# Constant products on TensorE ahead of long waits, host-laid weights and context, and a new step order in a one-core decoder layer

## What is computed

```python
x = x + attn(layernorm(x), gamma)        # softmax over -gamma * |xi - xj|^2, keys = values = the input itself
x = x + xattn(layernorm(x), ctx, ctx)    # 16 heads of width 8, alibi term slope_h * (i - j), Wq, Wk, Wv, Wo and biases
x = x + ffn(layernorm(x))                # 8 experts, the two with the largest router logits summed, W_e (128 x 128), b_e

mask = one_hot(top_k(softmax(h @ router_w.T + router_b), 2)).sum(-2)
out  = einsum('bse,ehd,bsd->bsh', mask, expert_w, h) + mask @ expert_b
```

## Time and profile before

| | |
|---|---|
| median of three runs | 304.29 us (303.43 to 306.56) |
| the profiled execution | 304.62 us, its span 302.8 us |
| instructions | 3232 |
| ScalarE, GpSimd busy | 111.9 us (37%), 61.6 us (20%) |
| DMA queues | 19.25 MB, 64 GB/s in the mean |

### The profile page before, as it was taken

How to read it: one execution, slowest core, us unless ns; L and a number is a source line. 1 busy time by engine, 2 the same in 40 slices (tenths; PEclk the granted TensorE clock), 3 DMA queues, 4 the chain that set the end, 5 groups by cost and what they waited for, 6 DMA issues and landing times.

```text
span 302.8 us, 3232 instructions
## 1 busy us (share of the span) xinstructions
PE 221.5 (73%) x1065; PEld 110.6 (37%) x1065; DVE 163.4 (54%) x405; ACT 111.9 (37%) x206; POOL 61.6 (20%) x114
## 2 busy tenths in 40 slices
PE   0858374688959899679989977987955799833194
PEld 0328251332823337623334663324334142223031
DVE  2167566379063678938476893825686240134060
ACT  1363351620155785145475415434102604500000
POOL 6160521200030000368000032800010250010080
PEclk9999788755589999959999996997985579995569
DMA  3790038500103510033532002451100400000521
GB/s 76 215 252 4 4 112 161 130 1 2 45 0 104 104 36 0 9 78 120 129 63 68 0 10 69 162 121 35 35 0 13 140 0 3 0 0 0 126 83 35
DMA packets 26409, 19.25 MB, mean 64 GB/s; under 512 B 12249, under 2 KB 25025, under 8 KB 26305
## 3 DMA queue, kind: packets, MB, share of 16 engines
q1 hardware_dynamic: 26393, 19.05, 24.5%
HBM read 13.64 MB, written 5.41 MB: 63 GB/s over the span
## 4 chain that ended last, share of the span: by engine, by line
PE 54%; DVE 22%; issue 9%; ACT 8%; DMA 3%; POOL 2%; SPq 0%; ACTq 0%; DVEq 0%; POOLq 0%
PE bank L1028 11%; PE bank L844 7%; DVE nm L752 6%; PE bank L986 5%; PE bank L887 5%; PE bank L984 5%; PE bank L943 5%; PE bank L904 4%; PE bank L964 3%; ACT pt L601 2%; PE bank L917 2%; DVE y L654 2%; DVE st L644 2%; PE bank L969 2%; ACT w L546 2%
## 5 line engine op out<-in xcount | busy, mean ns | idle before, releaser
L752 DVE TENSOR_REDUCE nm<-bank 128x3 f32<-128x462 f32 x88 | 50.3, 618 | 24.7 <-PE bank L943 23.6
L601 ACT ACTIVATE pt<-bank 128x512 f32<-128x512 f32 x80 | 44.1, 595 | 23.9 <-PE bank L964 11.0
L943 PE MATMUL bank<-kA,qs 128*128 128x308 bf16 (+1 forms) x172 | 33.0, 302 | 8.5 <-DVE nm L752 5.2
L436 POOL TENSOR_SCALAR ve<-mv 128x4 f32<-128x4 f32 x12 | 2.4, 204 | 174.4 <-DVE mv L647 174.3
L1028 PE MATMUL bank<-ym,ewT 128*128 128x512 f32 x64 | 32.4, 664 | 6.2 <-DVE ym L823 6.2
L823 DVE TENSOR_TENSOR ym<-mask_all,y3T 128x512 f32<-128x512 bf16 x16 | 21.6, 1409 | 26.6 <-DMA mask_all<-e_scratch 26.6
L512 POOL TENSOR_TENSOR ym<-mask_all,y3T 128x512 f32<-128x512 bf16 x16 | 25.5, 1624 | 40.1 <-DMA mask_all<-e_scratch 40.1
L964 PE MATMUL bank<-qs,kB 128*128 128x512 bf16 x64 | 26.0, 466 | 5.4 <-ACT pt L601 2.6
L887 PE MATMUL bank<-y1Tg,y1T 128*128 128x512 f32 x32 | 21.0, 746 | 7.9 <-ACT w L538 5.1
L844 PE MATMUL bank<-ident,y 128*128 128x128 f32 x48 | 10.9, 369 | 21.6 <-DVE y L654 21.1
L943 PEld LDWEIGHTS bank<-kA,qs 128*128 128x128 bf16 x172 | 13.9, 105 | 29.6 <-DVE nm L752 19.0
(11 more groups left out here) (145 smaller groups left out, 289.7 us busy)
## 6 DMA issues: line engine op xcount, KB each, us to landing
mask_all<-e_scratch SPq DMA_DIRECT2D x8, 512.0 KB, 4.8
qs<-q_scratch SPq DMA_DIRECT2D x8, 384.0 KB, 5.1
q_scratch<-qpart SPq DMA_DIRECT2D x4, 384.0 KB, 2.5
xs<-in_x_dram SPq DMA_DIRECT2D x4, 256.0 KB, 10.1
q_scratch<-qpart SPq DMA_DIRECT2D x4, 256.0 KB, 2.2
out_dram<-ob SPq DMA_DIRECT2D x4, 256.0 KB, 4.3
kA<-k_scratch SPq DMA_DIRECT2D x8, 120.0 KB, 3.9
kB<-k_scratch SPq DMA_DIRECT2D x8, 120.0 KB, 2.6
```

Source lines behind the costliest of these rows:

```text
L601: nc.scalar.activation(pt[:, n % PT_RING, :], ST[n % 2][:, :], ACT.Exp).then_inc(exps, 1)
L752: v.tensor_reduce(negated[:, GROUP * g:GROUP * g + heads], MX[n % 2][:, 0:heads * J].rearrange("p (s j) -> p s j", s=heads), AX.X, ALU.max ...
L943: last = mm(MX[n % 2][:, at * J:(at + heads) * J], qs[:, b % 2, a, tile(t)], kA[:, s:s + heads, a, 0:J], start=True, stop=True)
```

## The change

Four edits go together.

1. The host lays out the weights, biases and context as the matmuls want them. Five transfers take the place of the 18; the transposes, their copies and two memsets of padding are gone. The second element of x is loaded third, the expert weights and biases last.
2. The TensorE step `keys:0` stands directly behind `y1T:0` and waits for the weights and the context alone. VectorE's `weights:0` (memsets of the value and key buffers) stands ahead of `dist:0`.
3. In most TensorE steps the wait on free banks now comes first, then `warm(bank, step)`, then the wait on the data. `warm` issues products of a constant tile (128x128 by 128x512, bf16, all ones) into the bank that the step will overwrite. A table gives their number for 25 steps, 154 in all.
4. `ORDER` is another text for every engine.

```diff
+WARM = {
+    "y1T:0": 16, "probs:0": 12, "y2T:0": 16, "query:0": 4, "y1T:1": 5, "maxima:0": 13, "scores:0": 3, "y2T:1": 1,
+    "divide:0.0": 1, "y3T:0": 2, "mask:0": 8, "y2T:2": 3, "route:1": 3, "mask:1": 11, "scores:2": 1, "y3T:2": 5,
+    "route:2": 1, "mask:2": 5, "scores:3": 9, "experts:2": 1, "wo:3": 1, "y3T:3": 13, "mask:3": 4,
+    "experts:3": 14, "fT:3": 2,
 }
...
             load(xs[:, 0], x[0].rearrange("(t p) d -> p t d", p=P), x_in[0])
             load(gam[:, :], gamma.partition_broadcast(P), gamma_in)
...
+            load(xs[:, 1], x[1].rearrange("(t p) d -> p t d", p=P), x_in[1])
+            load(wT[:, :, :], proj, weights_in)
+            load(cols[:, :], rows, weights_in)
+            load(ctxT[:, :, :], ctxT_in, ctx_in)
             load(kA[:, :, :, :], k_aug[0], kaug_in)
             load(kB[:, :, :, :], k_aug[1], kaug_in)
...
+            load(ebin[:, :], expert_b, expert_in)
+            load(ewT[:, :, :], expert_w, expert_in)
...
             v = nc.vector
+            v.memset(idle[:, :], 1.0).then_inc(idle_set, 1)
...
         def _(pe):
             mm = nc.tensor.matmul
-            pe.wait_ge(consts, 5)
+            pe.wait_ge(idle_set, 1)
+
+            def warm(bank_, step):
+
+                for _ in range(WARM.get(step, 0)):
+                    mm(bank_[:, :], idle[:, 0:P], idle[:, :], start=True, stop=True)
...
-            def weights(b, _):
+            def keys(b, _):
                 pe.wait_ge(weights_in, W_LOADS * ONE)
-                pe.wait_ge(ctx_in, 5 * ONE)
-                turn(ST[0], lambda i: wraw[:, i, :])
-                turn(ST[1], lambda i: ewraw[:, i, :])
-                turn(MX[0], lambda i: ewraw[:, 4 + i, :])
-                nc.tensor.transpose(YV[:, 0:P], rwraw[:, :], ident[:, :])
-                turn(YM, lambda i: ctx_m[:, i, :])
-                for i in range(B):
-                    last = nc.tensor.transpose(MX[1][:, 32 * i:32 * i + 32], ctx_t[:, i, :], ident[0:32, 0:32])
-                last.then_inc(setup_ps, 1)
-
-            def keys(b, _):
-                pe.wait_ge(setup_sb, 6)
+                pe.wait_ge(ctx_in, ONE)
...
             def y2T_(b, _):
+                pe.wait_ge(pT_sb, T * (b + 1))
+                warm(A1, f"y2T:{b}")
                 pe.wait_ge(normed[1], b + 1)
-                pe.wait_ge(pT_sb, T * (b + 1))
                 turn(A1, lambda t: y2[:, t, :]).then_inc(y2T_ps, 1)
...
             def maxima(b, k):
                 if k == 0:
+                    if b == 0:
+                        pe.wait_ge(setup_sb, 2)
+                    if b >= 1:
+                        pe.wait_ge(mT_sb, b)
+                        pe.wait_ge(maxed, b * GROUPS)
+                    warm(MX[b * GROUPS % 2], f"maxima:{b}")
                     pe.wait_ge(kA_in, 2 * ONE * (b + 1))
                     pe.wait_ge(qs_in, 2 * ONE * (b + 1))
...
             def mask(b, _):
+                pe.wait_ge(y3T_sb, b + 1)
+                warm(YM, f"mask:{b}")
                 pe.wait_ge(mask_ready, b + 1)
                 turn(col16(YM), lambda t: maskp[:, t, :], ident16).then_inc(mask_ps, 1)
 
             def experts(b, _):
+                warm(YV, f"experts:{b}")
                 pe.wait_ge(mask_sb, b + 1)
                 if b == 0:
                     pe.wait_ge(bias_ready, 1)
```

More of the change, by code:

```diff
@@ L50 @@
     "scalar": """
[L51 to L60, removed]
@@ L66 @@
[L66 to L74, removed]
+        stats1:0 y1:0 weights:0 dist:0 rowmax:0 keys:0 gather:0 y2:0 stats1:1 y1:1 query:0 dist:1 rowmax:1
@@ L75 @@
+        divide:1.0 divide:1.1 maxima:2.8 maxima:2.9 wo:1 maxima:2.10 mcat:2 y3:1 gather:3 route:1 y2:3 select:1
+        query:3 store:1 divide:2.0 maxima:3.0 maxima:3.1 maxima:3.2 maxima:3.3 maxima:3.4 maxima:3.5 divide:2.1
+        maxima:3.6 maxima:3.7 wo:2 maxima:3.8 y3:2 maxima:3.9 maxima:3.10 mcat:3 route:2 select:2 store:2
+        divide:3.0 divide:3.1 wo:3 y3:3 route:3 select:3 store:3
     """,
     "tensor": """
-        y1T:0 dist:0 probs:0.0 probs:0.1 probs:0.2 probs:0.3 self:0 weights:0 y2T:0 query:0 keys:0 y1T:1 dist:1
@@ L78 @@
[L78 to L87, removed]
@@ L88 @@
-        maxima:2.10 probs:3.3 self:3 y3T:1 mT:2 route:1 mask:1 scores:2.0 y2T:3 scores:2.1 query:3 scores:2.2
-        scores:2.3 scores:2.4 scores:2.5 experts:1 scores:2.6 values:2.0 values:2.1 scores:2.7 maxima:3.0 fT:1
-        scores:2.8 maxima:3.1 scores:2.9 maxima:3.2 scores:2.10 divide:2.0 scores:2.11 maxima:3.3 values:2.2
-        maxima:3.4 values:2.3 maxima:3.5 divide:2.1 maxima:3.6 aoT:2 maxima:3.7 wo:2 maxima:3.8 maxima:3.9 y3T:2
+        y1T:0 keys:0 dist:0 probs:0.0 probs:0.1 probs:0.2 probs:0.3 self:0 y2T:0 query:0 y1T:1 dist:1 maxima:0.0
@@ new lines @@
+        probs:2.1 divide:0.1 probs:2.2 maxima:1.9 aoT:0 maxima:1.10 wo:0 probs:2.3 mT:1 self:2 y3T:0 scores:1.0
+        route:0 scores:1.1 scores:1.2 mask:0 y2T:2 query:2 scores:1.3 scores:1.4 y1T:3 scores:1.5 scores:1.6
+        experts:0 dist:3 maxima:2.0 values:1.0 maxima:2.1 fT:0 scores:1.7 maxima:2.2 values:1.1 maxima:2.3
+        probs:3.0 scores:1.8 maxima:2.4 scores:1.9 maxima:2.5 scores:1.10 maxima:2.6 scores:1.11 values:1.2
+        maxima:2.7 values:1.3 divide:1.0 maxima:2.8 divide:1.1 probs:3.1 aoT:1 probs:3.2 maxima:2.9 wo:1
@@ L94 @@
-        scores:3.11 values:3.2 values:3.3 divide:3.1 aoT:3 wo:3 y3T:3 route:3 mask:3 experts:3 fT:3
-    """,
+        experts:2 values:3.0 scores:3.6 values:3.1 scores:3.7 fT:2 scores:3.8 scores:3.9 scores:3.10 scores:3.11
+        values:3.2 values:3.3 divide:3.0 divide:3.1 aoT:3 wo:3 y3T:3 route:3 mask:3 experts:3 fT:3
+    """,
+}
+WARM = {
[4 rows of a table added]
 }
@@ L1007, in y3T_ @@
             def y3T_(b, _):
+                warm(YM, f"y3T:{b}")
                 pe.wait_ge(normed[2], b + 1)
```

175 lines of the change are left out of this document (95 added, 80 removed).

## The result

The changed kernel takes **294.76 us** (median of 4 runs, 294.32 to 296.19) against 305.05 for the kernel before, measured beside it (303.43 to 306.56). The ratio is 0.967, 95% interval 0.961 to 0.974. The gain is 10.3 us; the forecast was 22.6 us and its range ended at 291. The profiled execution took 294.3 us, with a span of 292.2. In this document the ratios leave out executions more than 1.5% above the fastest of their kernel and the medians keep them; without them the medians would be lower by 0.4 us (no products), 0.5 (order before), 0.2 (memsets early), 0.7 (tail order) and 1.2 (first 70 products).

A forecast was written before the change was run, and what follows sets the result against it. TensorE, busy 221.5 of 302.8 us with 96 us at half clock, was taken as the bound, besides setup and a few waits. Terms summed to -22.6 us (14.6 clock, 8 order and setup): 282.0 us, range 273 to 291.

The forecast's parts named there:

- Start to y2T:0: Kernel start through y2T:0: no gain, -1 to +3 us; key products hide under the memsets, first row maximum at 14.65.
- Rival 4: At the start, the inputs or the memsets hold back dist:0: +3 us, 285; chance 0.05.
- From the start to query:1: Everything up to query:1's end: done 14.8 us earlier, with the 22 maxima ending at 64.0.
- The scores of element 0 to self:2: From element 0's scores to self:2: +1.8 us, as values:0.2 waits for ScalarE's pvs; TensorE's work otherwise the same.
- Element 1: Stretch of element 1: -2 us, score products filling mask:0's wait of 3.18 us.
- element 2: Stretch of element 2: -5.0 us, from filled waits at mask:1 and ahead of maxima:3.0 and less half clock.
- Element 2's end: Route, y3T, ten scores and experts of element 2: -3.5 us, from full clock and scores bound by ScalarE.
- The clock term: Part of the forecast gain, over the whole kernel, that hangs on the clock: 14.6 us.
- Rival 1: In the maxima and self:1, the clock falls in thin stretches: costs 4.5 us, 286.5; chance 0.20.
- Rivals 2 and 6: Whole kernel: clock hardly holds, 296.6, chance 0.07; or constant operand cannot raise it, no chance of its own.
- rival 5: Whole kernel slower: constant products stand in front of ready work, a third uncovered, 317.6 us; chance 0.03.
- rival 3: No loss at values:0.2 and values:3.2, last experts at full clock: 276 us; chance 0.23.

The follow-up runs named there:

- no products: The changed kernel without any constant product, keeping its order, host layout and loads: 307.05 us, ratio 1.003 to the kernel before.
- order before: The changed kernel with the step order of the kernel before on all engines, keeping constant products and host layout: 299.44 us, ratio 0.976.
- memsets early: The changed kernel with VectorE's three long memsets moved into its idle time at the start: 291.72 us, ratio 0.954.
- tail order: The changed kernel with the order of the kernel before on TensorE and ScalarE from experts:2 on: 291.04 us, ratio 0.951.
- first 70 products: The changed kernel with only the 70 constant products up to y2T:1, the later 84 left out: 305.08 us, ratio 0.994.
- the copy first: The changed kernel with ScalarE's copy of values:0.1 (pvs) ahead of the four ReLUs of dist:2: 293.81 us, ratio 0.963.
- the order before in this place: The changed kernel with its new order up to query:1 and the order of the kernel before from there on: 287.85 us, ratio 0.942.
- the kernel with more products: New order to query:1 and self:3 to experts:2, old order elsewhere, early memsets, more constant products at y2T:0, y3T:3, mask:3, experts:3: 282.58 us, ratio 0.926.
- three moves: The changed kernel with early memsets, values:0.1's copy ahead of dist:2, and the order of the kernel before from experts:2 on: 286.86 us, ratio 0.941.

## Why the prediction was wrong, by its own steps

**Start to y2T:0** (0 forecast, +1.4 measured). The memsets were seen, and the first maximum was placed at 14.65 (15.19 measured). What was not followed is that a later first maximum makes TensorE wait, and that its clock then falls. Rival 4 (memsets hold back the start, +3 us) thus came true in part; taking the memsets out of the way gave 3.0.

**From the start to query:1** (-14.8, measured -14.6). Right in sum, by luck in part: the 1.4 us lost at the start are among the 14.6, so behind y2T:0 the kernel gained 16.0. The first maximum was 1.5 us late, and the 22 maxima with what stands between them ended 12.1 us later, where 13.7 had been counted (50.3 to 64.0). The split between clock and order was off too: without products the stretch is already 10.8 us shorter, against the 8.1 that the prediction left to the order; the products add 3.7, not 6.7.

**The scores of element 0 to self:2** (+1.8, measured +5.7). This is the first step that failed. It priced the `pvs` wait at its length (2.1 us, 2.08 measured) and stopped there. Moving the copy alone takes 3.7 us out of the stretch: 2.1 for the wait and 1.6 for the half clock behind it. Of the other 2.0 us, with the copy first, TensorE's waits are only 0.3 (1.5 before, 1.8 then) and the transposes of mT:1, which stood behind self:2 before, 0.4; the rest is longer busy time of TensorE (31.5 against 29.8 us in all, both at full clock), and its cause stays open. So "TensorE's work is the same" is not quite right for this stretch either. The queries from DRAM, the condition named at the prediction's end, come late only with the order before in this place (1.27 us); with them in time, in the kernel with more products, that order needs 32.2 us.

**Element 1** (-2, measured +1.2) and **element 2** (-5.0, measured -1.6). The waits that were to go did go, but others came. TensorE's waits in the kernel before from 124.3 to 177.4 us, and the same piece of work after, from 115.4 to 169.7 (us in total, times, longest):

```profile
PE bank L844 <- DVE maskp L813: 3.2, 1, 3.2
PE bank L844 <- DVE y L654: 0.5, 1, 0.5
PE bank L887 <- ACT w L538: 0.5, 1, 0.5
PE bank L964 <- ACT pt L601: 0.5, 2, 0.3
PE bank L844 <- DVE ao L775: 0.4, 1, 0.4
```

```profile
PE bank L952 <- ACT pt L584: 2.6, 3, 1.5
PE bank L974 <- ACT pvs L514: 1.7, 1, 1.7
PE bank L833 <- DVE ao L759: 1.0, 2, 0.5
PE bank L900 <- ACT y2T L514: 0.8, 1, 0.8
PE bank L952 <- DMA qs<-m_scratch: 0.6, 1, 0.6
```

These are the five largest of each. The mask wait of 3.2 us is gone, but where the other four sum to 1.9 us, the five of after sum to 6.7; over all releasers it is 6.0 before and 8.1 after. The new ones are waits for exponentials queued behind ScalarE's query work, for a `pvs` that ScalarE makes behind the last exponentials and the copy of probs:3.0, for other copies. With the order before in this place the stretch takes 52.9 us, 1.4 less. The stretch to wo:2 is alike, but milder: before, 3.2 for the mask, 2.8 for the queries and 2.7 in small ones; after, no wait above 0.8 us, but eight releasers whose waits add to 6.0, of which the largest three:

```profile
PE bank L952 <- ACT pt L584: 1.3, 3, 0.6
PE bank L928 <- DVE nm L736: 1.2, 5, 0.5
PE bank L974 <- ACT pt L584: 0.8, 1, 0.8
...
```

So 8.7 us of waits became 6.0, where the prediction let the mask and the query wait go and nothing come (part of the mask wait is now eleven constant products). The failed assumption is that a wait filled with useful work is won whole. The work that fills it comes from somewhere, and where it had stood, its followers now wait. That this holds for both stretches is read from the traces; no run took these small waits away one by one, so their single prices stay open. For element 2 the new order is still the better one by 2.7 us, as the run with the order before in that place shows (45.7 against 43.0).

**Element 2's end** (-3.5, measured -2.0): the clock fell in 216 to 219 us behind a wait of 2.23 us, and y3T:2 with five products ran at 1.2 GHz. Where it held, in the run with the tail's order of before, the stretch took 25.7 us, and 25.6 were forecast. (The term for the experts, 8.53 to 6.9 us, is 1.6 and not the 1.8 that was added; they took 7.30.) **Element 3** (+2.3, measured +2.9): right in kind. **The tail** (-1.4, measured -2.2): right in size by luck. From the last values product to the start of the last experts it takes 24.0 us, as before (23.9), so the 1.4 us counted for y3T, route and mask did not come. What came is the last experts at full clock, in 7.29 us against 9.65, which the prediction had only as possible and which the same 14 products did not bring in two other runs.

```profile
280.05 7.29 PE L1028 MATMUL bank<-ym,ewT 128*128 128x512 f32 x16 [1.69 <-DVE ym L807]
```

**The products' price and worth.** Thirteen took 2.97 us at full clock, 0.23 each, where 0.20 was forecast. The clock term, 14.6, measured 12.3. This kernel's runs do not agree with the Trainium skill's rule ("TensorE: Matmul & The Clock Gate", section "What's actually happening") that the ramp costs under 1% of a typical kernel's span: 12.3 us are 4% of it, in a kernel whose clock fell again and again. Rival 1 (the clock falls in the maxima) did not happen in the changed kernel's profiled execution (1.00 in 46 to 70 us), but its mechanism is real: in the runs with the memsets early, with three moves and with the order before, the clock fell inside the maxima behind the same 13 products. Why it held here and not there stays open. Rivals 2 and 6 fall by 0.951 and by the run without products, rival 5 by the gain itself; rival 3 asked for full clock and no loss at the two copies, and both copies cost.

The missing 12.8 us, then: 14.6 - 12.3 = 2.3 are the smaller clock term, and 8 + 1.7 = 9.7 are the order with the host layout, which was to gain 8 and by the run without products lost 1.7 (an interval that includes no change at all). The remaining 0.8 is within what the runs differ. Of the two parts only the order's is clear of the noise.
